# First feed-forward group of a Macaron block: magnitude sums of the down weights spread over later tiles, high parts ahead of signs, down product begun with six pairs

## The chip, the cores and the metric

The kernel runs on 1 core of one Trainium2 chip. The metric is the device time of one execution in microseconds (us). TensorE is called PE below, VectorE DVE, ScalarE ACT, GpSimd POOL, and SyncE (which issues the DMAs here) SP.

## The reference

The input is 2 x 2048 tokens of 512 numbers. Three residual layers follow one another: a feed-forward part, a state-space (Mamba) part, and the same feed-forward part again with the same weights. The change touches only the first feed-forward part:

```
def ternary_quant(w):
    scale = mean(|w|) + 1e-8
    return clip(round(w / scale), -1, 1) * scale      # value: scale times -1, 0 or 1
wu, wg, wd = ternary_quant(W_up), ternary_quant(W_gate), ternary_quant(W_down)   # 2048x512, 2048x512, 512x2048
up, gate   = x @ wu.T, x @ wg.T
hidden     = silu(up) * gate
x          = x + 0.5 * hidden @ wd.T                   # x inside is layer-normed
```

Each weight matrix needs the mean of its magnitudes before one of its values can be rounded.

## The kernel before, in words

The 4096 tokens are worked in 8 groups of 512. Group 0 is special, because the ternary weights are made while it runs. Group 1 uses the finished weights with plain products for up and gate. Groups 2 to 7 use a scheme of seven products. Then come the state-space part and the second feed-forward part, which nothing here touches.

**Up and gate of a group.** The 2048 hidden channels are 16 tiles of 128. For tile i PE computes up (8 matmuls of 512 columns) and gate (8 more), line 1117. ACT applies silu to the up result (`silu`, L633), DVE multiplies by the gate result (`hidden`, L860). PE's tile i waits for DVE's `hidden(i-2)`, since there are two result banks of each kind. Two tiles make a pair p (tiles 2p and 2p+1). ACT writes the 16-bit high part of a pair (`hid_high_direct`, L657), POOL subtracts it to get the low part (`low parts`, L528, two instructions for a pair). The buffer `h` holds two pairs, so `silu(i)` waits until POOL has finished pair i//2 - 2.

**Making the weights.** `TERNARY` lists 28 pieces. For a piece with a mask from ACT, ACT writes sign(w + half) into PSUM (`sign`, L596) and DVE combines it with (w > half) into the 8-bit weight (`combine`, L1032). For a piece in `OWN`, DVE writes the mask itself into SBUF (`mask`, L1021) and combines. Pieces 20 to 27 are those of the down weights; 21, 23, 25 and 27 are DVE's own. There are two mask buffers for ACT, so a sign waits for the combine two signs back. `T_AFTER` says how many pieces come after each tile i, on ACT and on DVE. The magnitude sum of a quarter of 2048 columns is one ACT instruction with an accumulator (`abs_sum`, L575); for the down weights there are four, after tiles 1 to 4. Then PE adds over the partitions (`weight_sum(2)`, L1296, called from `last_sum`), and DVE turns this into the thresholds and scales (`weight_scale(2)` and what follows, seven small instructions, called from `last_weights`). The order of every queue is written by hand; nothing but the order and the semaphores schedules anything.

**The order in group 0.** For each i, ACT does: silu(i) (from i = 4 on), the signs of the pieces after i, the magnitude sum where there is one, the high part of pair i/2 - 1 if i is even. DVE does: hidden(i), the pieces of i (before them the scales where due), the statistics of the next group after tiles 8 and 10.

**Down product of group 0.** Four token tiles of 128, `down_tile_of(t, p0, p1)`, L1184: for each pair 8 matmuls of 256 columns. The first two tiles run over pairs 0 to 6, then each over pair 7, then tiles 2 and 3 over all pairs. It waits for the low parts of the pairs it uses and for all 28 pieces.

**Behind it.** After pair 7 POOL makes four sums of the down weights (`t_sums`, L503) and ten of the sixteen sums of the up and gate weights (`s_sum`, L516), in one unbroken row, and only then reaches pair 0 of group 1. In group 1 DVE makes four sums for each pair (`pair_sums`, L387, L388, L394, L396), whose high and low parts ACT (L663, L669) and POOL (L493) take; these sums read two operands in SBUF.

Of the kernel before, what the change touches and what calls it, by code (L numbers as in the profile page):

```python
# [21 lines left out]
ALU = mybir.AluOpType  # L22
ACT = mybir.ActivationFunctionType
AX = mybir.AxisListType
# [16 lines left out]
HT, HE, HK = TG // 2, D // 2, KE // 2  # L41
# [4 lines left out]
def macaron_kernel(nc, u, w_up, w_gate, w_down, w_in, w_out, conv_w, conv_b, head_par, out):  # L46
# [14 lines left out]
    with top:  # L61
# [62 lines left out]
        def ffn_part(tag, first):  # L124
            ctx = ExitStack()
            with ctx:
# [111 lines left out]
                def raw_q(w, q):  # L238
                    if w == 2:
# [10 lines left out]
                           + [(0, 2, 256, 512), (1, 0, 256, 512), (1, 2, 256, 512)]  # L250
                           + [(w, q, n, n + 256) for n in (0, 256) for q in (1, 3) for w in (0, 1)]
                           + [(2, q, n, n + HE) for q in range(4) for n in (0, HE)])
                N_TERN, T_EARLY, T_AFTER = len(TERNARY), 9, (1, 1, 1, 1, 1, 2, 1, 2, 1, 2, 1, 2, 1, 1, 1, 0)

                OWN = [n for n, (w, q, e0, e1) in enumerate(TERNARY) if n < 5 or (w == 2 and e0)]

# [145 lines left out]
                with nc.Block() as block:  # L402
# [163 lines left out]
                    def _(act):  # L566
                        start_counts(act, [xnh_done, sil_done, hhi_done, u1_done, u2_done, c5_done, rh_done]
                                     + ([xhi_done] if first else []), done_before)
                        def abs_sum(w, q, n=2048):

                            at = (q if w < 2 else 3) * 2048
                            act.wait_ge(raw_in[4 * w + q], 16)
                            if w:
                                act.wait_ge(abs_done, 4 * (w - 1) + q + 1 if w < 2 else 4 * w + q)
                            nc.scalar.activation(flat_hi[:, at:at + n], raw_q(w, q)[:, 0:n], ACT.Abs,  # L575
                                                 accum_out=wsum[:, w, q:q + 1]).then_inc(abs_done, 1)

# [73 lines left out]

                        def hid_high_direct(p):
                            if p == 3:
                                act.wait_ge(abs_done, 12)
                            for i in range(2):
                                act.wait_ge(hid_done[i], after(p + 1))
                            nc.scalar.activation(hhi[:, p, 0:4, :], h[:, p % 2, :, :], ACT.Copy).then_inc(hhi_done, 2)  # L657
# [13 lines left out]
                        def direct_group():  # L671
                            for i in range(3):
                                silu(0, i)
                            sign(T_EARLY - 4)
                            silu(0, 3)
                            for n in range(T_EARLY - 3, T_EARLY):
                                sign(n)
                            for i in range(KE):
                                if i > 3:
                                    silu(0, i)  # L680
                                for n in pieces_after(i):
                                    if n not in OWN:
                                        sign(n)
                                if 1 <= i <= 4:
                                    abs_sum(2, i - 1)
                                if i and i % 2 == 0:
                                    hid_high_direct(i // 2 - 1)
                            hid_high_direct(HK - 1)
                            high_rows(1, 0, CH)

# [77 lines left out]
                    def _(dve):  # L768
# [122 lines left out]
                        def direct_group(between):  # L891
                            for i in range(KE):
                                hidden(0, i)
                                between(i)
                                if i in (8, 10):
                                    stats(1, i - 8)
                                    stats(1, i - 7)
                                if i == 12:
                                    dve.wait_ge(stat_done, after(2 * CH))
                                    dve.wait_ge(sil_done, after(i + 1))  # L900
                                    variance(1)
# [95 lines left out]
                        def abs_half(w, q):  # L997
# [3 lines left out]
                            nc.vector.tensor_reduce(wsum[:, w, at:at + 1], raw_q(w, q)[:, 1024:2048], AX.X, ALU.add,  # L1001
                                                    apply_absolute_value=True).then_inc(abs_half_done, 1)

                        def weight_scale(w):
                            dve.wait_ge(sum_done, w + 1)
                            step(nc.vector.tensor_reduce(total[:, w:w + 1], scale_bank(w), AX.X, ALU.add))
# [28 lines left out]

                        def last_weights(e):

                            if e == 8:
                                weight_scale(2)
                                whole_scale(2)  # L1040
                                step(nc.vector.tensor_tensor(prod[:, 0:1], scale[:, 0:1], scale[:, 1:2], ALU.mult))
# [38 lines left out]
                    def _(pe):  # L1080
# [111 lines left out]
                        def direct_group(between):  # L1192
                            for i in range(5, KE):
                                up_gate(0, i)
                                between(i)
                            for t in range(2):
                                down_tile_of(t, 0, HK - 1)
                            for t in range(2):
                                down_tile_of(t, HK - 1, HK)
                            for t in range(2, CH):  # L1200
                                down_tile_of(t, 0, HK)

# [87 lines left out]
                            pe.wait_ge(const_done, 3)  # L1290
                        if first:
                            def weight_sum(w):
                                pe.wait_ge(abs_done, 4 * w + 4)
                                if w < 2:
                                    pe.wait_ge(abs_half_done, 2 + w)
                                nc.tensor.matmul(scale_bank(w), ones[:, :], wsum[:, w, 0:PARTIAL[w]],  # L1296
                                                 start=True, stop=True).then_inc(sum_done, 1)

                            def last_sum(i):
                                if i == 8:  # L1300

                                    pe.wait_ge(tern_done, 1 + pieces_after(7)[-1])
                                    weight_sum(2)

                            for k in range(KD):
# [905 lines left out]
```

## Time and profile before

| | us |
|---|---|
| median of 3 runs | 1810.19 (1808.9 to 1812.73) |
| the profiled execution, its own time | 1809.33 |
| its span | 1807.0 |
| PE busy | 1755.3 (97%) |
| DVE, ACT, POOL busy | 1329.1, 926.8, 825.6 (74%, 51%, 46%) |

The granted PE clock is full in all 40 slices. The time outside the span is 2.3 us. Group 0 (with loading) takes the first 112.7 us of the span, group 1 ends near 209. A timeline row has: start in the span, duration, engine, line, operation, what is written <- what is read, partitions x elements, count; in square brackets the engine's idle time before it and what ended it. The page's first slice (45 us) has PE at 6 tenths, all others at 9 but the last.

### The profile page before, as it was taken

To read this page: it belongs to the slowest core of one execution; us is meant where nothing else is said; L and a number is where in the kernel's file an instruction comes from. 1 tells how busy PE (TensorE), PEld (TensorE's weight loads), DVE (VectorE), ACT (ScalarE), POOL (GpSimd) and SP (SyncE) were. 2 spreads that over 40 slices of the span, in tenths; PEclk is the share of its full clock that TensorE was granted. 3 is DMA by queue.
4 is the path that set the end of the run, shared out by engine and by line. 5 is a ranking of instruction groups with operands and counts; after the bars stand their busy time and mean duration, and the time that the engine had idled before them with its cause. 6 is when DMAs were issued, how large, how long until landed. Compare 5 with 4: busy or idle time off the path is not lost. (4 is left out here: it accounts for less than half of the span.)

```text
span 1807.0 us, 35150 instructions
## 1 busy us (share of the span) xinstructions
PE 1755.3 (97%) x13070; PEld 1266.9 (70%) x13070; DVE 1329.1 (74%) x2294; ACT 926.8 (51%) x1391; POOL 825.6 (46%) x553
## 2 busy tenths in 40 slices
PE   6999999999999999999999999999999999999998
PEld 3465888888888844444444444555888888888887
DVE  6838887778875857786786786657787778877655
ACT  7614457465473545445445445435447465474553
POOL 0496444363353515555455455536244362452533
PEclk9999999999999999999999999999999999999999
DMA  7032121311114030212212211111121311112100
GB/s 325 1 94 42 47 42 47 87 41 47 47 41 140 0 102 26 63 36 61 61 35 61 61 35 44 54 64 42 47 42 47 87 39 48 41 47 64 41 24 23
DMA packets 132968, 103.82 MB, mean 57 GB/s; under 512 B 100880, under 2 KB 100880, under 8 KB 131088
## 3 DMA queue, kind: packets, MB, share of 16 engines
q1 hardware_dynamic: 132880, 102.81, 18.9%
q8 instruction: 35, 0.57, 0.1%
q14 instruction: 53, 0.43, 0.1%
HBM read 49.59 MB, written 25.17 MB: 41 GB/s over the span
## 5 line engine op out<-in xcount | busy, mean ns | idle before, releaser
L493 POOL TENSOR_TENSOR f_hlo<-f_h,f_hhi 128x768 f16<-128x768 f32 x135 | 201.9, 1496 | 616.5 <-ACT f_hhi L663 588.3
L1146 PE MATMUL f_down_ps<-wd,f_hhi 128*128 128x256 fp8e4 x1440 | 318.5, 273 | 3.1 <-DVE xa L872 3.1
L1146 PE MATMUL f_down_ps<-wd,f_hlo 128*128 128x256 fp8e4 x1440 | 318.5, 273 | 0.0
L1219 PE MATMUL f_gate_ps<-spare 128*128 128x256 f16 x2496 | 306.2, 272 | 0.2 <-issue 0.2
L1219 PEld LDWEIGHTS f_gate_ps<-spare 128*128 128x128 fp8e4 x2496 | 236.2, 97 | 41.5 <-issue 0.4
L1219 PE MATMUL f_up_ps<-spare,wu 128*128 128x256 f16 x1664 | 213.5, 273 | 0.1
L872 DVE SCALAR_TENSOR_TENSOR xa<-f_down_ps,out_scale,xa 128x512 f32<-128x512 f32 x195 | 136.3, 743 | 60.3 <-PE f_down_ps L1146 60.0
L1219 PEld LDWEIGHTS f_up_ps<-spare,wu 128*128 128x128 fp8e4 x1664 | 160.2, 98 | 21.6 <-issue 0.3
L1146 PEld LDWEIGHTS f_down_ps<-wd,f_hhi 128*128 128x128 f16 x1440 | 140.6, 98 | 21.9 <-issue 5.1
L1591 POOL TENSOR_TENSOR s_am<-s_tri,s_al 128x512 f16<-128x512 f16 x128 | 153.1, 1225 | 6.1 <-DVE s_al L1851 6.1
L1146 PEld LDWEIGHTS f_down_ps<-wd,f_hlo 128*128 128x128 f16 x1440 | 140.7, 98 | 16.2
L493 POOL TENSOR_TENSOR f_hlo<-late,f_hhi 128x1024 f16<-128x1024 f32 x68 | 148.6, 2185 | 0.0
L1973 PE MATMUL s_wide<-xnt,late 128*128 128x512 f32 x320 | 145.3, 597 | 2.2 <-ACTq L115 1.5
L1798 DVE SCALAR_TENSOR_TENSOR s_xc<-s_xpad,late,s_xc 128x512 f32<-128x512 f32 x120 | 120.8, 1006 | 22.1 <-ACT s_xc L1660 19.3
L953 DVE SCALAR_TENSOR_TENSOR f_h<-f_h,hid_scale,f_tr_ps 128x512 f32<-128x512 f32 x104 | 77.4, 744 | 69.3 <-ACT f_h L713 69.3
L2103 PE MATMUL s_out<-late,s_yv 128*128 128x512 f32 x256 | 115.2, 593 | 0.0
L493 POOL TENSOR_TENSOR f_hlo<-spare,f_hhi 128x1024 f16<-128x1024 f32 x52 | 110.8, 2130 | 0.0
L947 DVE TENSOR_TENSOR f_tr_ps<-f_gate_ps,spare 128x512 f32<-128x512 f32 x104 | 72.7, 699 | 50.3 <-PE f_gate_ps L1219 50.3
L708 ACT ACTIVATE f_h<-f_up_ps,silu_scale 128x512 f32<-128x512 f32 x104 | 71.4, 687 | 72.8 <-PE f_up_ps L1219 72.8
L1219 PE MATMUL f_tr_ps<-spare 128*128 128x256 f16 x832 | 107.8, 273 | 0.2 <-DVE late L846 0.2
L1219 PE MATMUL f_gate_ps<-spare,wg 128*128 128x256 f16 x832 | 107.8, 273 | 0.0
L663 ACT ACTIVATE f_hhi<-f_h 128x768 f16<-128x768 f32 x120 | 97.1, 809 | 20.9 <-DVE f_h L960 19.1
(241 smaller groups left out, 3302.6 us busy)
## 6 DMA issues: line engine op xcount, KB each, us to landing
res<-xa SPq DMA_DIRECT2D x16, 1024.0 KB, 4.3
xa<-res SPq DMA_DIRECT2D x16, 1024.0 KB, 5.4
xa<-in_u SPq DMA_DIRECT2D x8, 1024.0 KB, 5.6
xa<-res SPq DMA_DIRECT2D x32, 256.0 KB, 2.6
res<-xa SPq DMA_DIRECT2D x32, 256.0 KB, 2.0
spare<-in_w_up SPq DMA_DIRECT2D x4, 1024.0 KB, 10.6
late<-in_w_gate SPq DMA_DIRECT2D x4, 1024.0 KB, 17.9
late<-in_w_in SPq DMA_DIRECT2D x1, 2320.0 KB, 8.7
```

The source lines that it names most:

```text
L493: last = nc.gpsimd.tensor_tensor(hlo[:, p, a:b, :], src, hhi[:, p, a:b, :], ALU.subtract)
L663: nc.scalar.activation(hhi[:, p, 0:n, :], h[:, p % 2, 0:n, :], ACT.Copy).then_inc(hhi_done, 1)
L708: nc.scalar.activation(h[:, p % 2, 0:2, :], two(A_ps[p % 2][:, :]), ACT.Silu, scale=silu_scale[:, 0:1]).then_inc(sil_done, 1)
L872: nc.vector.scalar_tensor_tensor(dst, src, out_scale[:, 0:1], dst, ALU.mult, ALU.add)\
L947: nc.vector.tensor_tensor(G_ps[:, :], C_ps[:, :], p5_sb, ALU.add).then_inc(c22_done, 1)
L953: nc.vector.scalar_tensor_tensor(at, at, hid_scale[:, 0:1], two(G_ps[:, :]), ALU.mult, ALU.mult)\
L1146: last = nc.tensor.matmul(at, part[:, p, kind, m * P:(m + 1) * P], wd[:, weight, p, :], start=(p == 0 and part is hhi and (m == 0 or name ...
L1219: last = nc.tensor.matmul(acc[:, j * HT:(j + 1) * HT], w[:, k, e * P:(e + 1) * P], xop[part][:, o, k, :, :], start=(fresh and (j, k, part) ...
L1591: last = nc.gpsimd.tensor_tensor(am[:, part, 4 * r:4 * r + 4, :], tri16[:, :].unsqueeze(1).to_broadcast([P, H // 2, P]), al[:, g[1], part, ...
L1798: nc.vector.scalar_tensor_tensor(xc[:, b, blk, :], xpad[:, t:t + TG], cvw[:, blk, t:t + 1], xc[:, b, blk, :], ALU.mult, ALU.add).then_inc( ...
L1973: last = nc.tensor.matmul(acc[:, :], win[:, k, row:row + P], xnt[:, k, :], start=(k == 0), stop=(k == KD - 1))
L2103: last = nc.tensor.matmul(out_ps[:, :], yv[:, k, :], wout[:, k, :], start=(k == 0), stop=(k == KD - 1))
```

## The change

`T_AFTER` moves pieces of the down weights one tile earlier from tile 10 on, so that piece 27 comes after tile 13. On ACT the high part of a pair goes ahead of the signs of the same i; the magnitude sums of the down quarters 0, 2 and 3 come after tiles 1, 5 and 7, and quarter 1 is one new DVE instruction of 2048 columns after tile 4 (`abs_whole`). `weight_sum(2)` and the scales come after tile 9 instead of 8. The first two tiles of the down product run over pairs 0 to 5, then each over pairs 6 and 7. The rest follows from these (semaphore counts).

```diff
-                N_TERN, T_EARLY, T_AFTER = len(TERNARY), 9, (1, 1, 1, 1, 1, 2, 1, 2, 1, 2, 1, 2, 1, 1, 1, 0)
+                N_TERN, T_EARLY, T_AFTER = len(TERNARY), 9, (1, 1, 1, 1, 1, 2, 1, 2, 1, 2, 2, 2, 1, 1, 0, 0)
@@ ACT, abs_sum
-                                act.wait_ge(abs_done, 4 * (w - 1) + q + 1 if w < 2 else 4 * w + q)
+                                act.wait_ge(abs_done, 4 * (w - 1) + q + 1 if w < 2 else 4 * w + max(q - 1, 0))
@@ ACT, hid_high_direct
-                                act.wait_ge(abs_done, 12)
+                                act.wait_ge(abs_done, 11)
@@ ACT, direct_group, for i in range(KE)
                                 if i > 3:
                                     silu(0, i)
+                                if i and i % 2 == 0:
+                                    hid_high_direct(i // 2 - 1)
                                 for n in pieces_after(i):
                                     if n not in OWN:
                                         sign(n)
-                                if 1 <= i <= 4:
-                                    abs_sum(2, i - 1)
-                                if i and i % 2 == 0:
-                                    hid_high_direct(i // 2 - 1)
+                                if i in (1, 5, 7):
+                                    abs_sum(2, {1: 0, 5: 2, 7: 3}[i])
@@ DVE, direct_group
                                 hidden(0, i)
                                 between(i)
+                                if i == 4:
+                                    abs_whole(2, 1)
@@ DVE
+                        def abs_whole(w, q):
+                            dve.wait_ge(raw_in[4 * w + q], 16)
+                            nc.vector.tensor_reduce(wsum[:, w, q:q + 1], raw_q(w, q), AX.X, ALU.add,
+                                                    apply_absolute_value=True).then_inc(abs_half_done, 1)
@@ DVE, last_weights
-                            if e == 8:
+                            if e == 9:
                                 weight_scale(2)
@@ PE, direct_group
-                                down_tile_of(t, 0, HK - 1)
+                                down_tile_of(t, 0, HK - 2)
                             for t in range(2):
-                                down_tile_of(t, HK - 1, HK)
+                                down_tile_of(t, HK - 2, HK)
@@ PE, weight_sum and last_sum
-                                pe.wait_ge(abs_done, 4 * w + 4)
-                                if w < 2:
-                                    pe.wait_ge(abs_half_done, 2 + w)
+                                pe.wait_ge(abs_done, (4, 8, 11)[w])
+                                pe.wait_ge(abs_half_done, 2 + w)
-                                if i == 8:
-
-                                    pe.wait_ge(tern_done, 1 + pieces_after(7)[-1])
+                                if i == 9:
+
+                                    pe.wait_ge(tern_done, pieces_after(8)[-1])
```

## Rows read from the trace of the kernel before

**Rows 1.** Windows: group 0 up to its down product; busy time of each engine, clock, DMA
```profile
0.00:84.63 84.63, 62.99 (x278) 29.17 (x279) 65.66 (x101) 60.13 (x73) 20.57 (x23) 1.00 0.43 174
```
**Rows 2.** Timeline, PE, group 0: where it waits
```profile
40.07 1.89 PE L1117 MATMUL f_up_ps<-xnt,wu 128*128 128x512 f16 x8
...
45.26 1.89 PE L1117 MATMUL f_up_ps<-xnt,wu 128*128 128x512 f16 x8 [1.57 <-DVE f_h L860]
...
49.72 1.89 PE L1117 MATMUL f_up_ps<-xnt,wu 128*128 128x512 f16 x8 [0.84 <-DVE f_h L860]
...
57.62 0.39 PE L1296 MATMUL f_down_ps<-wsum,ones 128*128 128x4 f32 x2 [0.84 <-DVE wu L1032]
...
78.75 1.89 PE L1117 MATMUL f_up_ps<-xnt,wu 128*128 128x512 f16 x8
80.47 1.89 PE L1117 MATMUL f_gate_ps<-xnt,wg 128*128 128x512 f16 x8
...
84.63 0.27 PE L1184 MATMUL f_down_ps<-wd,f_hhi 128*128 128x256 fp8e4 x1 [2.27 <-POOL f_hlo L528]
...
98.74 0.28 PE L1184 MATMUL f_down_ps<-wd,f_hhi 128*128 128x256 fp8e4 x1
```
**Rows 3.** Timeline, ACT, group 0: one of each kind of instruction
```profile
34.97 1.90 ACT L575 ACTIVATE f_hhi<-f_hlo 128x2048 f16<-128x2048 f32 x1
...
47.17 1.04 ACT L657 ACTIVATE f_hhi<-f_h 128x1024 f16<-128x1024 f32 x1
48.12 0.67 ACT L633 ACTIVATE f_h<-f_up_ps,silu_scale 128x512 f32<-128x512 f32 x1
48.69 1.11 ACT L596 ACTIVATE f_down_ps<-spare,half 128x1024 f32<-128x1024 f32 x1
```
**Rows 4.** Timeline, DVE, group 0
```profile
26.27 1.21 DVE L1001 TENSOR_REDUCE wsum<-late 128x1 f32<-128x1024 f32 x1
...
58.21 0.15 DVE L1006 TENSOR_REDUCE total<-f_down_ps 128x1 f32<-128x4 f32 x1
...
59.41 1.28 DVE L1032 SCALAR_TENSOR_TENSOR wg<-late,half,f_tr_ps 128x1024 fp8e4<-128x1024 f32 x1
60.60 1.28 DVE L776 BATCH_NORM_STATS2 f_stat<-xa 128x6 f32<-128x512 f32 x2
...
66.50 0.74 DVE L860 SCALAR_TENSOR_TENSOR f_h<-f_h,hid_scale,f_gate_ps 128x512 f32<-128x512 f32 x1
...
70.98 1.28 DVE L1032 SCALAR_TENSOR_TENSOR late<-xn,half,spare 128x1024 fp8e4<-128x1024 f32 x1
...
75.39 2.06 DVE L1032 SCALAR_TENSOR_TENSOR wd<-spare,half 128x1024 fp8e4<-128x1024 f32 x1
```
**Rows 5.** Timeline, POOL, end of group 0 and the row of sums behind it
```profile
80.50 3.73 POOL L528 TENSOR_TENSOR f_hlo<-f_h,f_hhi 128x512 f16<-128x512 f32 x2 [1.46 <-ACT f_hhi L657]
85.11 2.27 POOL L528 TENSOR_TENSOR f_hlo<-f_h,f_hhi 128x512 f16<-128x512 f32 x2 [0.89 <-ACT f_hhi L657]
...
118.30 3.97 POOL L516 TENSOR_TENSOR spare<-wg 128x1024 fp8e4<-128x1024 fp8e4 x2
124.78 1.65 POOL L493 TENSOR_TENSOR f_hlo<-f_h,f_hhi 128x768 f16<-128x768 f32 x1 [2.51 <-ACT f_hhi L663]
```
**Rows 6.** Timeline, group 1: DVE's first pair sums, the hidden tile behind them, PE
```profile
121.39 1.17 DVE L387 TENSOR_TENSOR late<-f_h 128x256 f32<-128x256 f32 x1
...
124.80 0.73 DVE L860 SCALAR_TENSOR_TENSOR f_h<-f_h,hid_scale,f_gate_ps 128x512 f32<-128x512 f32 x1
...
134.21 1.89 PE L1117 MATMUL f_up_ps<-xnt,wu 128*128 128x512 f16 x8 [0.60 <-DVE f_h L860]
```
**Rows 7.** Timeline, state-space part: four POOL instructions in a row beside queued DVE ones
```profile
707.44 4.73 POOL L1591 TENSOR_TENSOR s_am<-s_tri,s_al 128x512 f16<-128x512 f16 x4
...
709.75 1.52 DVE L1911 TENSOR_TENSOR s_yv<-s_yv,s_zs 128x512 f32<-128x512 f32 x1
711.20 1.01 DVE L1829 TENSOR_SCALAR s_sp<-s_dtv 128x32 f32<-128x32 f32 x1
```

## The prediction

> **What bounds the kernel now.** I read the page first: PE is busy for 97% of the span, and the chain that ended last is PE's to nearly its whole length. So a change can only win where PE waits, or lose by making it wait. The slices put the one thin place of PE in the first 45 us, and the windows of group 0 [rows 1] show 63.0 us of PE in 84.6, with DVE at 65.7 and ACT at 60.1. Of the rest, 20 us are loading and start, before the change's first edit. The timeline of PE [rows 2] shows what the change can reach: 1.57 us ahead of tile 6 and 0.84 ahead of tile 7 (hidden tile from DVE late), 0.84 ahead of the partition sum, 2.4 between the last gate product (80.47 + 1.73 = 82.20) and the down product (84.63), and 0.14 where the third token tile begins (98.74, though 14 steps of 0.875 and two more end at 98.60). A last wait of 0.17 stands ahead of tile 15. In all about 6.0 us, 0.33% of the kernel. That is the ceiling of the win.
>
> Why the first two waits: tile 6 waits for hidden(4), which waits for silu(4), which stands on ACT behind three magnitude sums of 1.89 each [rows 3]. Why the 2.4: the low part of pair 6 takes POOL 3.73 instead of 2.27 [rows 5], next to DVE's mask and own combine.
>
> **The port.** An own combine takes 2.06 us where POOL works and 1.28 where it doesn't [rows 4], and POOL's pair 2.27 or up to 3.73 [rows 5]. DVE's and POOL's instructions that read two SBUF operands exclude each other. The Trainium skill (SBUF — State Buffer, "Who interferes with whom") calls this an exclusive lock on a shared port pair, held for the whole instruction; by that rule, the trace agrees. When both have a queue they take turns: POOL's four instructions take 4.73 and two queued DVE ones, 0.69 and 0.2 long when free, take 1.52 and 1.01 [rows 7], held up 0.8 each. So three DVE sums in a row beside a busy POOL cost up to one POOL instruction each.
>
> **The change part by part.** Durations are those of rows 3 to 5; on one engine the next instruction begins some 0.08 before the end of the last (59.41 + 1.28 against 60.60), ACT's steps are 1.04 for a sign, 1.89 for a magnitude sum, 0.97 for a high part, 0.59 for a silu. PE's product steps on after 1.73 (78.75 to 80.47 in rows 2), a tile after 3.45. I laid the queues out from 33 us on with these; the same layout with the old order puts the waits of rows 2 within 0.3 us.
>
> *Tiles 2 to 5.* High part 0 now stands ahead of sign 11, so at 36.86 (34.97 + 1.89 in rows 3) ACT does 0.97 of it first. Sign 11, 1.1 long, ends at 38.9 instead of 37.96, DVE's combine 11 begins 38.95, hidden(3) ends 40.9 instead of 39.93, and up of tile 5 begins 41.0 instead of 40.07: a new wait of 0.95.
>
> *Tiles 6 to 9.* POOL's pair 0 ends at 40.2 instead of 43.2, silu(4) runs at 40.3 and hidden(4) ends 42.7, before PE wants it (44.5). The new reduce has 2048 columns, twice the 1.21 of rows 4, less one start: 2.3. It lies at 44.3 to 46.6, hidden(5) ends 47.3, PE wants it at 47.9. So 1.57, 0.84 and the 0.84 of the sum (now behind tile 9, no wait) are gone, and up of tile 10 begins 58.5, 2.8 earlier than before. That a reduce could be held by POOL no row shows; up to +1.1 would go to hidden(5) and cost some 0.3 in the end, below nothing it can't go. By the same page of the Trainium skill a tensor_reduce never contends; then it would be 0.
>
> *ACT.* From silu(5) at 44.7 (gate 5 ends 44.6) the queue up to sign 19 is four silus, five signs, two magnitude sums, two high parts: 2.36 + 5.20 + 3.78 + 1.94 = 13.3. Sign 19 begins 58.0, and DVE's combine 19 59.1, where it was 59.41. Thus DVE comes to its heavy part no earlier, while PE is 2.8 earlier. This is the point that decides.
>
> *DVE, tiles 9 to 15.* From 59.1: combine 19 (1.19), statistics (1.25), hidden(9) (0.66); then the scales, and since sign 20 can only begin with the threshold, 0.5 (three small ones as at 58.21, and the handover) + 1.1 until combine 20 may start (before, the sign ran ahead of it); combine 20 (1.19), mask 21 (0.8), combine 21 (1.2, and 0.7 for the port, as POOL does pair 4 then). Hidden(10) begins 67.75 and ends 68.5. PE, after a wait of 0.4 at tile 11, wants it at 65.9: 2.8 of waiting. Tile 10 now has an own piece and the statistics: 0.66 + 1.19 + 0.8 + 1.2 + 1.25 = 5.1, against PE's 3.45: hidden(11) ends 73.6, another 1.6. Tile 11: 0.66 + 1.19 + 0.8 + 1.2 + 0.7 (port, pair 5) = 4.6: another 1.1. Tile 12 is lighter, no wait at 15. Gate 15 begins 80.47 + 3.0 = 83.5. The port terms: neither held is -1.4; the mask held too is +0.6.
>
> *Down product.* Pair 5 is ready near 78.5, piece 27 at 82.4, so it begins at 85.2, at once; against 84.63 that is +0.6. Pair 7's low part is done at 90.3, six pairs last to 95.7. Tile 0 now ends two steps of 0.875 ahead of tile 1, which hides DVE's 0.75: -0.14. PE enters group 1 0.45 us later than before.
>
> *POOL behind it.* Its row of sums begins after pair 7, thus 3.0 later (90.3 against 87.4), and PE only 0.45: POOL is 2.5 later against PE. It had 2.5 of idle time before pair 0 of group 1 [rows 5], so its own work is just in time. But DVE's first pair sums (121.39 in rows 6, now 121.8) met only the tail of POOL's last sum, 0.76 us. Now two more POOL instructions of 1.97 lie there, and pair 0's low part. Taking turns, the first sum is held 1.5, the second 1.8, the third 1.4, and hidden(2) begins 129.1 instead of 124.80. PE's tile 4 begins 3.0 later than its shifted place; the wait of 0.60 ahead of tile 6 [rows 6] goes. Net +2.4. Ends of this term: 0 (if DVE's sums go through as one, the first wait falls into statistics and slack) and +3.6 (if POOL's small power instruction holds the port its full time).
>
> From there all is the same work with the same distances: group 1's down product, the groups of seven and the rest shift as a whole. Sum: 0.45 + 2.4 = +2.8 us. Against this profile's 1809.33 that is 1812.1; this execution lies 0.9 below the median of its runs, so for a median I say 1813.0. A difference below 0.2%, 3.6 us, can't be told from no change here. The likeliest case is thus no measurable difference, on the slow side; its own range is 1810.5 to 1815.
>
> **The rivals.** *DVE keeps pace (faster).* If hidden(10) is there by 65.7, the waits of tiles 12 to 14 stay away: tiles win 3.4 - 0.95, the down product 2.4 and 0.14, sum -5.0. For it: DVE idles some 4 us between 49 and 59 in my layout, and what it waits for are single signs on ACT. Against it: DVE has the new 2.3 and, for tiles 9 to 11, 15 us of work in 10.4 of PE. But POOL would be 2.5 later against PE here too, since it hangs on tile 15 and the down product doesn't any more; with that loss it is -2.6, and only without it -5.0, 1805. Chance 0.17, two thirds of it beyond 3.6 us.
>
> *The port decides (slower).* Place: DVE's pair sums 0 and 1 of group 1 against POOL's sums. It decides once POOL is over 1.5 us later against PE. All four sums of pair 0 and the first of pair 1 are held, +3.6, and with the mask of piece 25 held in tile 11 (+0.6) and the reduce (+0.3) it comes to +4.5 to +5: 1815. For it: single instructions were held 1.7 in group 1. Chance 0.30.
>
> *No loss in group 1.* DVE's sums pass, or POOL is early: +0.45, 1810.6. Chance 0.13. My forecast has 0.40.
>
> **How the numbers follow.** Faster by over 0.2%: 0.12 (from the first rival). Slower: 0.32 (the second, and the upper edge of the forecast). The rest, 0.56, is within. The range reaches from half the first rival, -3.7, to the second with its surcharge, +5.8.
>
> **What would show it.** Right: waits of PE ahead of tiles 5, 12, 13 and 14 (0.95, 2.8, 1.6, 1.1) in place of 6 and 7; gate 15 near 83.5; the down product without a wait; combine 19 near 59.1; POOL's sums beginning near 90.3; DVE's L387, L388 and L394 near 122 to 127 long, and PE waiting some 3 ahead of tile 4 of group 1. Wrong: gate 15 before 80, or group 1 lasting the 58.1 us from 112.72 to its down product that it has now.

## The result and the profile after

The changed kernel takes 1813.99 us (median; 1812.19 to 1816.43), the kernel before 1810.19: the ratio is 1.0019, with a 95% interval of 1.0011 to 1.0028. Both medians are of 12 executions. It is slower by 3.8 us by the medians (0.21%) and by 3.4 us by the ratio, whose interval reaches from 2.0 to 5.1 us: small, at the edge of what I had said could be told from no change, but clear of it. The profiled execution after took 1814.8 us (span 1812.4), 0.8 above its median, where that of before lay 0.9 below its own. So the two spans differ by 5.4 us, 1.7 more than the medians. Part of the surplus lies in the state-space part, 554.9 us long here and 552.8 before: the same code, whose length in the profiled executions of this study goes from 552.7 to 554.9. Of those 2.1 us no experiment shows the cause. The sharper yardstick is therefore where group 2 begins:

| us from the span's start | before | after |
|---|---|---|
| down product of group 0 begins | 84.63 | 84.83 |
| group 1 begins | 112.72 | 112.78 |
| down product of group 1 begins | 170.82 | 174.51 |
| group 2 begins | 198.09 | 201.78 |
| groups 2 to 7 | 446.41 | 446.12 |

The loss of 3.7 us is there, and it all comes in the 58.10 us between the second and the third line, which became 61.73. Nothing was won ahead of it. (Group 2 begins at 198.09 in the kernel before; the end of group 1 "near 209" that I gave above is wrong.)

Two lines of the page of the changed kernel, PE's and DVE's busy time over the span:

```profile
span 1812.4 us, 35148 instructions
...
PE 1757.1 (97%) x13070; PEld 1267.6 (70%) x13070; DVE 1335.0 (74%) x2295; ACT 925.1 (51%) x1389; POOL 825.0 (46%) x553
```

DVE is 5.9 busier than before (1329.1). The new reduce is 2.28 of that. Three held instructions of group 1, shown below, take 3.9 more than before (5.86 against 1.17, 0.41 and 0.41).

The timeline of PE after, where it waits (the column behind the start is the duration; the rows of before are [rows 2]):

```profile
40.58 1.89 PE L1124 MATMUL f_up_ps<-xnt,wu 128*128 128x512 f16 x8 [1.02 <-DVE f_h L860]
...
61.81 1.89 PE L1124 MATMUL f_up_ps<-xnt,wu 128*128 128x512 f16 x8 [0.22 <-DVE f_h L860]
...
68.08 3.27 PE L1124 MATMUL f_up_ps<-xnt,wu 128*128 128x512 f16 x8 [2.66 <-DVE f_h L860]
71.19 1.89 PE L1124 MATMUL f_gate_ps<-xnt,wg 128*128 128x512 f16 x8
73.10 1.89 PE L1124 MATMUL f_up_ps<-xnt,wu 128*128 128x512 f16 x8
...
77.93 1.89 PE L1124 MATMUL f_up_ps<-xnt,wu 128*128 128x512 f16 x8 [1.21 <-DVE f_h L860]
...
84.83 0.27 PE L1191 MATMUL f_down_ps<-wd,f_hhi 128*128 128x256 fp8e4 x1
...
129.61 3.22 PE L1124 MATMUL f_up_ps<-xnt,wu 128*128 128x512 f16 x8 [2.85 <-DVE f_h L860]
```

The waits of 1.57, 0.84 and 0.84 of [rows 2] are gone, and so is the 2.27 ahead of the down product. In their place stand 1.02 (tile 5), 2.66 (tile 12) and 1.21 (tile 14). Two rows are not 1.89 long but 3.27 and 3.22: the eight matmuls of tile 12 in group 0 and of tile 4 in group 1, each the first behind its longest wait. The windows of two of these stretches (columns as in [rows 1]; the seventh number, after POOL's, is the granted clock) show what PE's clock did:

```profile
66.00:68.00 2.00, 0.00 (x0) 0.00 (x0) 2.00 (x3) 1.31 (x2) 2.00 (x2) 0.87 0.00 0
68.00:70.00 2.00, 1.92 (x5) 0.74 (x6) 1.97 (x3) 0.00 (x0) 0.29 (x1) 0.50 0.00 0
...
130.00:132.00 2.00, 2.00 (x6) 0.72 (x5) 1.91 (x4) 0.00 (x0) 2.00 (x2) 0.50 0.00 0
```

PE ran there at 0.50, which is the lower of the two levels, 1.2 GHz, after it had done nothing for 2.66 and 2.85 us. That was nowhere in my sum, and it could have been: the row of nines on the page means 90% or more in slices of 45 us and hides such a fall. "Full in all 40 slices", as I wrote, is more than it says. The kernel before has two of them, in its state-space part (PE's row and the window of the first):

```profile
1123.74 1.82 PE L2074 MATMUL s_mix<-s_lx,s_dtx 128*64 128x128 f32 x16 [2.65 <-DVE s_dtx L1879]
...
1122.00:1128.00 6.00, 4.26 (x35) 2.97 (x36) 3.55 (x6) 0.17 (x1) 4.29 (x5) 0.72 0.23 62
```

DVE after: the stretch that makes tile 12 late, and in group 1 the sums of the first pair ([rows 4] and [rows 6] before):

```profile
43.84 2.28 DVE L1008 TENSOR_REDUCE wsum<-xn 128x1 f32<-128x2048 f32 x1
...
58.54 1.28 DVE L1039 SCALAR_TENSOR_TENSOR wg<-late,half,f_tr_ps 128x1024 fp8e4<-128x1024 f32 x1 [1.21 <-ACT f_tr_ps L596]
...
65.29 1.99 DVE L1039 SCALAR_TENSOR_TENSOR late<-f_hlo,half,spare 128x1024 fp8e4<-128x1024 f32 x1
67.20 0.73 DVE L860 SCALAR_TENSOR_TENSOR f_h<-f_h,hid_scale,f_gate_ps 128x512 f32<-128x512 f32 x1
...
74.84 2.28 DVE L1039 SCALAR_TENSOR_TENSOR wd<-spare,half 128x1024 fp8e4<-128x1024 f32 x1
...
121.44 1.78 DVE L387 TENSOR_TENSOR late<-f_h 128x256 f32<-128x256 f32 x1
123.15 2.22 DVE L388 TENSOR_TENSOR late<-f_h 128x256 f32<-128x256 f32 x1
125.30 1.86 DVE L394 TENSOR_TENSOR late<-late,f_h 128x256 f32<-128x256 f32 x1
127.19 0.42 DVE L396 TENSOR_TENSOR late<-f_h,late 128x256 f32<-128x256 f32 x1
128.73 0.73 DVE L860 SCALAR_TENSOR_TENSOR f_h<-f_h,hid_scale,f_gate_ps 128x512 f32<-128x512 f32 x1
```

POOL after ([rows 5] before): its row of sums begins at 89.98, and the last two stand where DVE wants to begin.

```profile
89.98 3.83 POOL L503 TENSOR_TENSOR wd<-late,wd 128x2048 fp8e4<-128x2048 fp8e4 x1
...
120.93 4.16 POOL L516 TENSOR_TENSOR spare<-wg 128x1024 fp8e4<-128x1024 fp8e4 x2
125.05 1.82 POOL L493 TENSOR_TENSOR f_hlo<-f_h,f_hhi 128x768 f16<-128x768 f32 x1
128.78 2.13 POOL L493 TENSOR_TENSOR f_hlo<-late,f_hhi 128x1024 f16<-128x1024 f32 x1 [1.91 <-ACT f_hhi L669]
```

DVE's three sums are each 0.42 long when free. The second and the third end 0.3 us behind a POOL instruction that was ahead of them. POOL has none of the 2.51 of idle time that it had in [rows 5].

### The profile page after: what moved, and what is told of

Same layout as the page of the kernel before. It is cut to its first block and busy times, and to the rows that moved or that the text cites. A ratio compares the mean times of both kernels' runs of the same rounds, so it can differ in the third digit from the quotient of the medians.

```text
span 1812.4 us, 35148 instructions
## 1 busy us (share of the span) xinstructions
PE 1757.1 (97%) x13070; PEld 1267.6 (70%) x13070; DVE 1335.0 (74%) x2295; ACT 925.1 (51%) x1389; POOL 825.0 (46%) x553
```

## Experiments

Each ratio is to the kernel before, on the same chip; x1 to x4, x5 to x8 and x9 to x11 ran on three chips, so times across these groups are compared by the ratios. "Group 2 at" is from the profiled execution (198.09 before, 201.78 after).

**Seven pairs first (x1).** One part undone:

```diff
-                                down_tile_of(t, 0, HK - 2)
+                                down_tile_of(t, 0, HK - 1)
...
-                                down_tile_of(t, HK - 2, HK)
+                                down_tile_of(t, HK - 1, HK)
```

> The changed kernel with the down product of the first two token tiles again begun with seven pairs; all else as changed. Theory (POOL's row of sums too late against PE): the down product waits for pair 6 again and PE enters group 1 1.2 us later than in the changed kernel, but POOL is then only 1.4 us late against PE instead of 2.6, DVE's first pair sums are held once and not three times, and group 1 takes 58.3 to 58.6 us instead of 61.7: 1811.9 in all, 2.1 faster than the changed kernel. Rival (the loss lies in tiles 10 to 12 alone, and the earlier down product is a pure gain): 1.2 slower than the changed kernel, 1815.2.

Measured: 1812.46 us, ratio 1.0012 (1.0003 to 1.0021), group 2 at 199.55. PE in x1:

```profile
68.22 1.89 PE L1124 MATMUL f_up_ps<-xnt,wu 128*128 128x512 f16 x8 [2.66 <-DVE f_h L860]
...
73.24 1.89 PE L1124 MATMUL f_up_ps<-xnt,wu 128*128 128x512 f16 x8 [1.41 <-DVE f_h L860]
...
77.85 1.89 PE L1124 MATMUL f_up_ps<-xnt,wu 128*128 128x512 f16 x8 [0.99 <-DVE f_h L860]
...
85.87 0.27 PE L1191 MATMUL f_down_ps<-wd,f_hhi 128*128 128x256 fp8e4 x1 [0.96 <-POOL f_hlo L528]
```

Windows of x1, the stretch behind the 2.66:

```profile
68.00:70.00 2.00, 1.78 (x9) 0.87 (x10) 1.97 (x4) 0.00 (x0) 0.43 (x1) 1.00 0.00 0
```

With seven pairs PE waits 0.96 for pair 6, as the change says it would, and enters group 1 1.2 later; but group 1 then takes 58.32 instead of 61.73. Beginning earlier was no gain: what PE won ahead of group 1 brought it closer to POOL's row of sums. And here the same wait of 2.66 left the clock at 1.00. Of the 3.41 us by which group 1 is shorter, 1.2 are the clock's, which did not fall there either (see x6).

**Eight sums in the row (x2).** POOL makes eight instead of ten sums of the up and gate weights before group 1:

```diff
-S_EARLY = 10
+S_EARLY = 8
```

> The changed kernel with POOL doing 8 instead of 10 sums of the up and gate weights before group 1 (the other two come with the last ones, behind group 1). Theory: POOL is free 3.9 us earlier, before DVE's first pair sums, so L387, L388 and L394 of pair 0 take 0.4 us each, PE doesn't wait ahead of tile 4 of group 1, its clock stays full there, and group 1 takes 58.0 us: 3.7 faster than the changed kernel, 1810.3. Tiles 2 to 15 of group 0 are as in the changed kernel. Rival (two sums more behind group 1 cost as much, or the wait in group 1 has another cause): 1814.

Measured: 1813.57 us, 1.002 (1.0008 to 1.0031), group 2 at 200.45; 3.3 above the expectation, a miss. The stage was as expected: group 1 lasts 58.08 until its down product. But that product takes 30.34 instead of 27.27, the rival's case. DVE, PE and the windows of x2 there:

```profile
189.91 2.54 DVE L846 SCALAR_TENSOR_TENSOR late<-spare,late 128x768 f16<-128x768 f32 x1
```
```profile
195.48 0.37 PE L1153 MATMUL f_down_ps<-wd,f_hhi 128*128 128x256 fp8e4 x1 [2.72 <-DVE xa L872]
```
```profile
195.00:200.00 5.00, 4.52 (x28) 3.47 (x29) 4.97 (x11) 1.81 (x3) 0.00 (x0) 0.66 0.00 0
```

The two sums left out of the row were made behind pair 7 of group 1, beside DVE's L846 (0.95 long when free, 2.54 here), which reads two SBUF operands as well. The clock fell behind the 2.72 too. The collision was moved, not removed. That the first loss hangs on the row is shown; that it could be had back was not, until x9.

**Six pairs alone (x3)**, in the kernel before:

```diff
-                                down_tile_of(t, 0, HK - 1)
+                                down_tile_of(t, 0, HK - 2)
```

(and HK - 2 in the second call).

> The kernel before with only the down product's edit (six pairs, then two). Theory: piece 27 now ends the wait (83.3 us), so the down product begins 1.0 to 1.3 us earlier and 0.14 more is won at the third token tile, POOL is 1.1 to 1.4 late against PE, which group 1 bears with 0 to 0.4: 1809.2, 1.0 faster than before. Rival (any lateness of POOL costs its full size): no gain, 1810.2.

Measured: 1808.96 us, 0.9993 (0.9984 to 1.0001), group 2 at 196.72. By itself this part is worth about a microsecond, hardly more than the interval can tell: the down product starts at 83.07, after 1.00 of waiting for piece 27 instead of 2.27 for POOL.

**Spread sums alone (x4).** The changed kernel with seven pairs, the old `T_AFTER` and signs ahead of high parts, so that only the magnitude sums, the partition sum and the scales are moved.

> The kernel before with only the magnitude sums spread (after tiles 1, 5 and 7 on ACT, one on DVE after tile 4) and the partition sum and scales after tile 9; pieces, high parts and the down product as before. Theory: the waits ahead of tiles 6, 7 and the partition sum go (3.2 us), DVE's heavy stretch costs 1 to 1.5 of it at tiles 12 to 14, gate 15 begins 1.7 us earlier than before, and POOL is not late against PE: 1808.3, 1.9 faster than before. Rival (the spreading itself is what overloads DVE): slower than before, 1811 or more.

Measured: 1809.0 us, 0.999 (0.9981 to 0.9999), group 2 at 196.72. Again about a microsecond won: waits of 0.27, 1.19 and 0.34 among the tiles, then 1.74 ahead of the down product.

**Pieces where they were (x5).** The changed kernel with the old `T_AFTER`:

```diff
-(1, 1, 1, 1, 1, 2, 1, 2, 1, 2, 2, 2, 1, 1, 0, 0)
+(1, 1, 1, 1, 1, 2, 1, 2, 1, 2, 1, 2, 1, 1, 1, 0)
```

> The changed kernel with the pieces of the down weights after the same tiles as before (one piece after tile 10, the last after tile 14). Theory: hidden(11) has an own piece less in front of it, the wait at tile 13 shrinks, gate 15 begins 1.5 us earlier, and the down product waits for piece 27 again (84.6 to 85.0), so PE's shift is about the same but POOL is not late: group 1 58.3 us instead of 61.7, in all 3.7 faster than the changed kernel, 1810.3. Rival (the pieces' place is indifferent, since the same work waits): 1814.

Measured: 1811.61 us, 1.0006 (0.9997 to 1.0014), group 2 at 199.20; 1.3 above what was expected. The wait at tile 12 is the same 2.66, again with a low clock behind it (rows of 2.52 and 2.99); the down product waits 0.96 for piece 27, and group 1 takes 58.48.

**Signs first (x6).** The changed kernel with the high part behind the signs again:

```diff
-                                if i and i % 2 == 0:
-                                    hid_high_direct(i // 2 - 1)
                                 for n in pieces_after(i):
...
+                                if i and i % 2 == 0:
+                                    hid_high_direct(i // 2 - 1)
```

> The changed kernel with the signs ahead of the high parts on ACT again. Theory: the wait of 1.0 ahead of tile 5 goes, sign 19 begins 1 us earlier, so DVE's heavy stretch does too and the wait at tile 12 falls from 2.7 to about 1.5, which also leaves the PE clock full there; gate 15 begins 2.5 us earlier, PE's shift stays in group 1 as POOL is as late against PE as in the changed kernel: 2.5 faster than the changed kernel, 1811.5. Rival (high parts first pay, since POOL starts earlier): 1814 or slower.

Measured: 1812.24 us, 1.001 (0.9998 to 1.0021), group 2 at 198.28. The 1.02 at tile 5 is gone, as is more than half of the 2.66 (the waits are 0.27 ahead of tile 7 and 1.20, 1.57 and 0.99 ahead of tiles 12 to 14), and group 0 is 2.25 shorter. Group 1 takes 60.55. The time is 0.7 above the expectation. Its PE row and windows:

```profile
127.35 1.89 PE L1124 MATMUL f_up_ps<-xnt,wu 128*128 128x512 f16 x8 [2.85 <-DVE f_h L860]
```
```profile
128.00:130.00 2.00, 2.00 (x11) 0.94 (x10) 1.91 (x3) 0.00 (x0) 2.00 (x2) 1.00 0.00 0
```

This is the cleanest measure of the port's share: the same 2.85 of waiting as after the change, no low clock, 60.55 - 58.10 = 2.45 us lost. The rest of 61.73, 1.2 us, is the clock's. That is so in the profiled execution, whose mean clock over the span was 0.998; in the other eleven of x6 it lay between 0.996 and 0.998.

**A wait for each bank (x7).** PE's up product needs only silu(i-2) to be done (it frees the up bank), its gate product hidden(i-2). Before, one wait stood ahead of both.

```diff
+                            if i > 1:
+                                pe.wait_ge(sil_done, after(KE * g + i - 1))
+                            else:
+                                pe.wait_ge(hid_done[i % 2], after(HK * g + i // 2))
                             up_or_gate(i, 0)
+                            if i > 1:
+                                pe.wait_ge(hid_done[i % 2], after(HK * g + i // 2))
                             up_or_gate(i, 1).then_inc(ug_done, 1)
```

> The changed kernel with PE's wait for hidden(i-2) moved from before the up product of tile i to before its gate product; the up product waits only for silu(i-2), which is what frees its bank. Theory of the clock (a wait of PE of 2.7 and 2.9 us is what halved the granted clock behind it): no wait is over 2.1 us, the clock stays at full, up of tiles 12 of group 0 and 4 of group 1 take 1.89 and not 3.2, and with the 1.7 us hidden behind each wait the kernel is 3.9 to 5 faster than the changed one, 1809.5. Rival (the fall of the clock has nothing to do with the wait before it): low-clock stretches of about 3 us stay, 2 us faster at most, 1812.

Measured: 1808.15 us, 0.9993 (0.998 to 1.0006), group 2 at 197.67. PE's waits in x7, now ahead of the gate products of tiles 12, 13, 14, and of tile 4 of group 1:

```profile
67.42 1.90 PE L1129 MATMUL f_gate_ps<-xnt,wg 128*128 128x512 f16 x8 [1.23 <-DVE f_h L860]
...
72.44 1.90 PE L1129 MATMUL f_gate_ps<-xnt,wg 128*128 128x512 f16 x8 [1.39 <-DVE f_h L860]
...
77.05 1.90 PE L1129 MATMUL f_gate_ps<-xnt,wg 128*128 128x512 f16 x8 [0.98 <-DVE f_h L860]
...
126.91 1.90 PE L1129 MATMUL f_gate_ps<-xnt,wg 128*128 128x512 f16 x8 [1.02 <-DVE f_h L860]
```

The up product of 1.73 is done inside the old wait, so 2.85 became 1.02. No wait up to there is over 1.4 us, and no row of groups 0 and 1 is at a low clock. It is worth some 4.7 us against the changed kernel, going by the two ratios: group 1 begins 2.6 earlier and takes 60.22 instead of 61.73. The port still takes its share there (L387, L388 and L394 last 1.78, 2.22 and 1.85), and PE waits 1.52 for POOL ahead of group 1's down product.

**All that looked good by then (x8).** Waits for each bank, signs first, eight sums in the row, and pieces after tiles 9 to 15 as 1, 2, 2, 1, 2, 0, 0.

> The changed kernel with four edits: signs ahead of high parts, POOL's 8 sums before group 1, the pieces of the down weights after tiles 9 to 13 as 1, 2, 2, 1, 2 (the own piece away from the statistics of tile 10), and the split waits of PE. Theory: gate 15 begins 76.5 to 77, the down product near 80, group 1 takes 56.2, no low clock: 6 faster than before, 1804.2, and the second feed-forward part gives up to 2 more by the split. Rival (each removed wait comes back at the next one): within 2 us of the kernel before.

Measured: 1808.6 us, 0.9992 (0.9983 to 1.0), 4.4 above the expectation: a miss. Group 2 begins at 195.92. Group 1 was short (56.75), but its down product paid the 2.72 of x2 again (28.86), and piece 27 came late for that of group 0. PE and the windows of x8:

```profile
80.70 0.27 PE L1196 MATMUL f_down_ps<-wd,f_hhi 128*128 128x256 fp8e4 x1 [1.98 <-DVE wd L1039]
```
```profile
82.00:84.00 2.00, 2.00 (x11) 1.45 (x10) 1.75 (x3) 2.00 (x3) 0.88 (x1) 0.50 0.00 0
```

Here the low clock came after only 1.98 of waiting, and the stage lasted 29.61 instead of the 27.94 of x6: 1.7 us. Behind the 2.72 in group 1's down product it did not fall.

**Sums between the pairs (x9).** The changed kernel with eight sums in the row, and the other eight spread: one each after pairs 0, 1, 2, 4 and 7 of group 1, the last three behind.

```diff
-                                if first and p in (0, 1, HK - 1):
-                                    s_sum(S_EARLY + p % 5)
+                                if first and p in SUM_AT:                # (0, 1, 2, 4, HK - 1)
+                                    s_sum(S_EARLY + SUM_AT.index(p))
```

> The changed kernel with POOL's sums of the up and gate weights placed otherwise: 8 instead of 10 before group 1, and after the low parts of pairs 0, 1, 2, 4 and 7 of group 1 one each (as changed: pairs 0, 1 and 7), so that as many as before are left behind group 1. Theory (lateness of POOL costs through the port, and in the run with 8 sums the gain was given back in group 1's down product, where two sums more held DVE): group 1 takes 58.1 us as there, its down product 27.3 again, so group 2 begins 3.6 us earlier than in the changed kernel and at the place of the kernel before: 1810.3 in all. Rival (moved sums always cost their gain elsewhere): the two sums inside group 1 hold DVE there and group 1 takes 60 us or more, 1813.

Measured: 1809.03 us, 0.9997 (0.9987 to 1.0006), group 2 at 197.22: 4.6 earlier than after the change. Of these 3.65 are group 1's, which takes 58.08, and its down product takes 27.27 as before. The other 0.9 are no work of the edit: in group 0, which it does not touch and which has the 2.67 wait and the low clock again, the combine of piece 25 met POOL's low part otherwise and took 1.28 instead of 2.28, so that the down product began at 83.93 instead of 84.83. The same happened in x2 (84.09). So a port meeting can go either way in two executions of the same code, for 0.9 us. DVE and POOL of x9:

```profile
74.93 1.28 DVE L1039 SCALAR_TENSOR_TENSOR wd<-spare,half 128x1024 fp8e4<-128x1024 f32 x1
...
120.54 0.43 DVE L387 TENSOR_TENSOR late<-f_h 128x256 f32<-128x256 f32 x1
120.88 0.42 DVE L388 TENSOR_TENSOR late<-f_h 128x256 f32<-128x256 f32 x1
121.21 0.42 DVE L394 TENSOR_TENSOR late<-late,f_h 128x256 f32<-128x256 f32 x1
```
```profile
116.10 3.97 POOL L516 TENSOR_TENSOR spare<-wu,spare 128x1024 fp8e4<-128x1024 fp8e4 x2
123.93 1.64 POOL L493 TENSOR_TENSOR f_hlo<-f_h,f_hhi 128x768 f16<-128x768 f32 x1 [3.86 <-ACT f_hhi L663]
```

Once POOL's row ends before DVE's sums start, they take 0.43 and 0.42 instead of 1.78, 2.22 and 1.86. This settles the loss in group 1: with POOL's row out of the way it is gone whole, the wait of 2.85 and the low clock behind it included.

**A wait for each bank in the kernel before (x10).** The edit of x7 alone.

> The kernel before with only PE's split waits (up product waits for silu(i-2), gate product for hidden(i-2)). Theory: the waits of 1.57, 0.84 and in group 1 of 0.60, 0.81 and 0.81 go behind the up product, but in group 0 the last pieces and pair 6 set the down product at 84.4 anyway: group 0 unchanged, group 1 56.2 to 56.8 us instead of 58.1, and the same in the second feed-forward part: 3 faster than before, 1807.2. Rival (hidden tiles are late by DVE's whole load, so the wait only moves to the gate product): no gain, 1810.2.

Measured: 1809.44 us, 0.9997 (0.9988 to 1.0006): no difference that can be told, 2.2 above the expectation, though group 2 begins at 196.16, 1.9 earlier. PE of x10:

```profile
44.53 1.89 PE L1122 MATMUL f_up_ps<-xnt,wu 128*128 128x512 f16 x8 [0.91 <-ACT f_h L633]
...
84.46 0.27 PE L1189 MATMUL f_down_ps<-wd,f_hhi 128*128 128x256 fp8e4 x1 [2.27 <-POOL f_hlo L528]
```

Group 1 is 1.65 shorter (56.45), but in group 0 the waits are now for silu itself, late behind the magnitude sums on ACT, and the 2.27 for pair 6 stays. The second feed-forward part is no shorter than before (609.4 against 609.7), against the expectation. What became of the 1.9 is known for the profiled execution alone: its state-space part took 554.50 instead of 552.75, with a fall of the clock at 642.8. So x7's gain was for the most part the cure of an illness that the change had brought.

**All of it (x11).** The changed kernel with a wait for each bank, signs first, the sums of x9, ACT's magnitude sums after tiles 1, 3 and 5 instead of 1, 5 and 7, and the pieces after tiles 9 to 13 as 1, 2, 2, 2, 1.

```diff
-(1, 1, 1, 1, 1, 2, 1, 2, 1, 2, 2, 2, 1, 1, 0, 0)
+(1, 1, 1, 1, 1, 2, 1, 2, 1, 1, 2, 2, 2, 1, 0, 0)
...
-                                if i in (1, 5, 7):
-                                    abs_sum(2, {1: 0, 5: 2, 7: 3}[i])
+                                if i in (1, 3, 5):
+                                    abs_sum(2, {1: 0, 3: 2, 5: 3}[i])
```

> The changed kernel with: signs ahead of high parts, magnitude sums on ACT after tiles 1, 3 and 5, pieces of the down weights after tiles 9 to 13 as 1, 2, 2, 2, 1, split waits of PE, and POOL's sums as in the run with sums inside group 1. Theory: the down product begins near 79.5, POOL is late by no more than it can bear, group 1 takes 56.2 to 57, its down product 27.3, group 2 begins 6 to 7 us earlier than in the kernel before: 1804, and up to 2 less by the second feed-forward part. Rival (each wait that goes comes back as another): within 2 us of the kernel before.

Measured: 1800.96 us (1800.62 to 1801.96, five runs), 0.9951 (0.9938 to 0.9965): 9 us faster than the kernel before. It beats both, the changed one by some 12 us going by the two ratios. PE, DVE and the window of group 0 in x11:

```profile
76.84 1.90 PE L1129 MATMUL f_gate_ps<-xnt,wg 128*128 128x512 f16 x8 [0.41 <-DVE f_h L860]
78.92 0.27 PE L1196 MATMUL f_down_ps<-wd,f_hhi 128*128 128x256 fp8e4 x1 [0.17 <-DVE wd L1039]
```
```profile
56.12 1.28 DVE L1039 SCALAR_TENSOR_TENSOR wg<-late,half,f_tr_ps 128x1024 fp8e4<-128x1024 f32 x1
```
```profile
0.00:78.92 78.92, 62.16 (x279) 29.46 (x280) 64.27 (x99) 57.16 (x70) 18.98 (x22) 1.00 0.46 187
```

From 38 us to the down product PE waits 0.58 in all. Combine 19 starts at 56.12 instead of 58.54 and DVE has no idle time ahead of it: the third magnitude sum no longer stands between it and its sign on ACT. Group 2 begins at 190.85, 7.2 earlier than before; the other 0.6 of the two spans' difference lies behind it, and the time outside the span is 1.8 us instead of 2.3, as in the other kernels with a wait for each bank (x7, x8 and x10: 1.7 to 1.8). What each of the five edits gives of the 9 us was not taken apart.

## Why the prediction was right, and where a size was off

*Group 0, right in its steps.* The execution after runs 0.44 ahead of that of before from the start (hidden(0) at 33.16 against 33.60), which is to be added to its times.

| step | forecast | measured |
|---|---|---|
| wait, tile 5 | 0.95 | 1.02 |
| combine 19 | 59.1 | 58.54 |
| hidden(10) begins | 67.75 | 67.20 |
| waits, tiles 11, 12, 13, 14 | 0.4, 2.8, 1.6, 1.1 | 0.22, 2.66, none, 1.21 |
| gate 15 | 83.5 | 83.11 |
| down product, no wait | 85.2 | 84.83 |
| PE enters group 1 | +0.45 | +0.06 (+0.50 with the 0.44) |
| POOL's sums begin | 90.3 | 89.98 |

The deciding step was "DVE comes to its heavy part no earlier, while PE is 2.8 earlier". It held: sign 19 sat behind ACT's queue of four silus, five signs, two magnitude sums and two high parts. x11 is the counter-test: with a magnitude sum moved from tile 7 to 5 (and the order of x6), combine 19 comes 2.4 earlier (1.5 of it by the order alone, 57.05 in x6), and with the split waits and the other places of the pieces the waits nearly vanish. That also shows the first rival's condition, DVE keeping pace, to be reachable, by another order than the change's.

The one wait that is missing, 1.6 at tile 13, is no error of DVE's layout: PE spent 3.27 - 1.89 = 1.4 more on tile 12 at the low clock, and so came later to the next wait. In x1, where the clock stayed, the waits are 2.66, 1.41 and 0.99, as forecast within 0.2.

*Group 1, right in its mechanism.* I had forecast the three sums held by 1.5, 1.8 and 1.4; they were by 1.35, 1.80 and 1.44 (1.78, 2.22 and 1.86, less 0.43, 0.42 and 0.42 of x9). Hidden(2) begins at 128.73 (129.1), PE waits 2.85 (3). POOL's lateness, forecast as 2.5 against PE, was 2.8 by the overlaps below. The net loss was put at 2.4, and is 2.45 in x6. The Trainium skill (SBUF — State Buffer, "Who interferes with whom") says that whichever engine issues first has the shared pair for the whole instruction and the other is blocked meanwhile; by that rule each sum should end just behind the POOL instruction ahead of it, and the trace agrees: L388 ends at 125.37 and L394 at 127.16, POOL's row at 125.09 and its low part at 126.87. Which of the two issued first the starts in the rows do not always tell: the combine at 74.84 begins 0.05 ahead of POOL's pair 5 and is held 1.0 nonetheless. That page's rule that a tensor_reduce never contends could not be tried: POOL was at work beside the new reduce only for its first 0.1 us (43.84, 2.28 long).

How sharp the step is shows when the kernels are put in the order of the overlap, the end of POOL's row less the start of DVE's L387:

| kernel | row ends | L387 starts | overlap | group 1 to its down product |
|---|---|---|---|---|
| x9 | 120.07 | 120.54 | none | 58.08 |
| before | 122.27 | 121.39 | 0.9 | 58.10 |
| x4 | 122.17 | 119.84 | 2.3 | 58.29 |
| x1 | 125.01 | 122.63 | 2.4 | 58.32 |
| x3 | 122.17 | 119.68 | 2.5 | 58.45 |
| x5 | 124.63 | 122.11 | 2.5 | 58.48 |
| x6 | 122.84 | 119.19 | 3.65 | 60.55 |
| after | 125.09 | 121.44 | 3.65 | 61.73 |

Up to 2.5 us of overlap one sum is held, and DVE's slack takes all but 0.4 of it. At 3.65 three are, since POOL goes from its last sum straight into pair 0's low part, and 2.45 us come out. The rival's point, "over 1.5 us later", is thus too early: x4 and x3 are 1.4 to 1.6 us later than before and lost 0.2 to 0.35; the step lies between 1.6 and 2.8. The rest of that rival did not come: the mask of piece 25 (74.06) took 0.74, its free length.

*What was missing.* My sum had no term for PE's clock. In the profiled execution it added 1.2 us in group 1 (61.73 against 60.55; the row itself is 3.22 - 1.89 = 1.3 longer), and 1.4 in group 0, which cost little there because PE would have waited anyway. With it the forecast +2.8 becomes about +4, near the 3.7 at group 2. That the medians differ by 3.8 does not prove this term: the interval of 2.0 to 5.1 us holds +2.8 without it, and also the second rival's +4.5 to +5. It is the stages, not the time, that speak for the forecast. And the clock is not the same in every execution: over the span it was 0.995 on average in the profiled one, with five falls and the end, and from 0.994 to 0.998 in all twelve. Three had 0.998, as much as the kernel before with its two falls, and still took spans of 1811.3 to 1811.4, against 1807.0. So most of the loss does not seem to need a low clock behind the two waits; how often it fell just there is not known.

*Numbers of mine that were off.* "Half the first rival, -3.7" does not come out: half of its -5.0 is -2.5, and -3.7 is near the middle between its two values, -2.6 and -5.0. The upper end, +5.8, has a surcharge over +5 that I gave no row for. The measured time lies in the range either way.

*Part against part.* The six pairs alone and the spread sums alone are each worth about a microsecond (x3, x4). Together, with the high parts first and the pieces earlier, they lose 3.7 at group 2. The two without the other two were not tried. Neither of the two is slow in itself: each brings PE nearer to a POOL row that starts no earlier, and over the step above the gain is paid back more than once. That the high parts ahead of signs are a loss of their own is shown for group 0: its down product begins at 82.58 with the signs first (x6) and at 84.83 with the high parts first. For the pieces one tile earlier I have only x5, where the down product starts 0.67 later; its time is nonetheless 2.4 lower by the ratios, since PE came later to group 1 (113.44 against 112.78) and POOL's row ended earlier (124.63 against 125.09), so that the overlap stayed at 2.5. What that part is worth where POOL is no trouble was not measured.

## What to carry to other kernels

When the engine that bounds the kernel gains time in one stage, measure the distance to every engine that doesn't gain with it, and to the next place where it shares a port or a buffer with them; in these runs a win smaller than that distance was kept, and a larger one was turned into a new wait. Spread a long row of background work over the gaps between urgent instructions rather than finish it first (x9), and look at what it meets in its new place (x2). And let each product wait only for the bank that it writes: it cut a wait of 2.85 us to 1.02 (x7), and where no wait was that long it neither cost nor gained anything measurable (x10).

## What the runs showed of the hardware that I had not expected

PE's granted clock fell to 0.50 behind single waits of 2 to 3 us, for some 3 us: after 2.66 and 2.85 (after), 2.65 and 2.72 (x2), 2.66 (x5), 2.67 (x9) and 1.98 (x8). Eight matmuls of 512 columns then took 2.52 (x5, and the next eight 2.99) to 3.50 (x9) instead of 1.89; the two events in the changed kernel cost 1.4 and 1.3 us, those of x5, x8 and x9 1.6 to 1.7. But the same 2.66 in x1, 2.85 in x6 and 2.72 in x8, and the 2.27 of [rows 2], left it at 1.00, so the length of one wait does not decide by itself. Shorter ones can be enough: in x10 it fell with a wait of 1.51 (642.8), and in the kernel before with waits of 1.27 and 0.89 that follow each other (1154.7).

The kernel before shows the same in places that the change does not touch. Its wait of 2.65 in the state-space part, in the fence above, comes in every kernel; in eleven of the thirteen profiled executions the clock fell there, in two (after, x6) it did not. Behind a wait of 2.2 near 1203 it fell in four (x2, x3, x6, x8), and from the last product of the state-space part to the end of the span these executions took 611.1 to 611.3 us, against 609.4 to 609.7 in the nine others. So the same code with the same wait meets either case, at 1.3 to 1.7 us each, and the mean clock of the twelve executions of the changed kernel, 0.994 to 0.998, says so too. A single profile can't tell how often. What decides, these runs don't settle. From 38 us to the down product of group 0 no fall came in the kernels whose waits there were all under 1.8 us (x3, x4, x6, x7, x11).

DVE and POOL alternate at the port even where the DVE instruction is tiny: 0.42 us of work took 1.78 to 2.22, and L846 with 768 columns, 0.95 when free, took 2.54 beside a POOL sum (x2).
